# Alternating VectorE's steps over two batches in a four-stream decoder kernel, with gates spread straight from their column

## The reference

```python
def _layernorm(x, eps=1e-5):
    m, v = mean(x), var(x)
    return (x - m) / sqrt(v + eps)

# part "pick" (layer 0, ffn): half of the tokens are picked by their gates
gate = sigmoid((x @ Wg)[..., 0])
_, idx = top_k(gate, C)                       # C = 50 of 100
attn_in = take_along_axis(x, idx[..., None], axis=1)
...                                           # 16 heads over the 50 tokens
out = zeros_like(x).at[:, idx].set(o * gate_sel[..., None])

# part "quant" (layer 1, ffn)
x_norm = x * rsqrt(mean(square(x)) + 1e-6)
absmax = max(abs(x_norm), axis=-1)
scale = 127.0 / clip(absmax, 1e-5)
x_q = clip(round(x_norm * scale), -128, 127) / scale
y = einsum('bsd,od->bso', x_q, w_int8 * weight_scale) + bias

x = _layernorm(x + agent part(x))             # "mix"
x = _layernorm(x + cross attention(x, ctx))   # "first"
x = _layernorm(x + pick(x))                   # "pick"
x = _layernorm(x + banded attention(x))       # "local", 16 heads, band of 64
x = _layernorm(x + cross attention(x, ctx))   # "second"
x = _layernorm(x + quant(x))                  # "quant"
```

## Time and profile before

| | |
|---|---|
| Time, median of 3 runs (lowest to highest) | 1081.24 us (1078.39 to 1082.4) |
| Time of the profiled execution | 1081.67 us |
| Its span, first to last instruction | 1079.9 us |
| Mean granted TensorE clock over the span | 0.876 of 2.4 GHz |
| PE busy | 900.4 us (83%) |
| DVE busy | 704.7 us (65%) |
| ACT busy | 514.2 us (48%) |
| POOL busy | 371.4 us (34%) |

### The profile page before, as it was taken

How to read it: one execution, slowest core, us unless ns; L and a number is a source line. 1 busy time by engine, 2 the same in 40 slices (tenths; PEclk the granted TensorE clock), 3 DMA queues, 4 the chain that set the end, 5 groups by cost and what they waited for, 6 DMA issues and landing times.

```text
span 1079.9 us, 19738 instructions
## 1 busy us (share of the span) xinstructions
PE 900.4 (83%) x7022; PEld 671.0 (62%) x7022; DVE 704.7 (65%) x2081; ACT 514.2 (48%) x2392; POOL 371.4 (34%) x528
## 2 busy tenths in 40 slices
PE   7957798898798699998889788897979688997983
PEld 5735677565577587665567566574647466765662
DVE  4235666565777857567697876558487686766576
ACT  3102244766542345865433355664535144556641
POOL 0045401344463322254443422236144232223243
PEclk9766898999888799997889699898869898998896
DMA  7801400002214000002032200011030400000000
GB/s 227 285 32 44 157 1 2 2 8 85 92 55 144 24 1 2 2 23 73 30 123 75 78 9 2 12 69 34 11 102 1 144 17 1 1 2 1 1 1 31
DMA packets 23382, 54.10 MB, mean 50 GB/s; under 512 B 3696, under 2 KB 9588, under 8 KB 23284
## 3 DMA queue, kind: packets, MB, share of 16 engines
q1 hardware_dynamic: 23284, 52.84, 14.7%
HBM read 49.53 MB, written 3.31 MB: 49 GB/s over the span
## 4 chain that ended last, share of the span: by engine, by line
PE 50%; DVE 26%; ACT 10%; POOL 5%; issue 4%; DMA 4%; SPq 1%; DVEq 0%; POOLq 0%; ACTq 0%
PE psum L419 8%; PE psum L424 8%; PE psum L458 7%; ACT work L763 4%; PE psum L444 4%; DVE bn L878 4%; PE psum L578 4%; PE psum L589 3%; ACT work L728 3%; DVE x L885 3%; PE psum L599 2%; DVE mx L1040 2%; PE psum L581 2%; DVE res L945 1%; DVE mv L880 1%
## 5 line engine op out<-in xcount | busy, mean ns | idle before, releaser
L763 ACT ACTIVATE work<-psum,mx 100x100 f32<-100x100 f32 x512 | 169.8, 369 | 53.1 <-DVE mx L1040 52.8
L1124 POOL TENSOR_SCALAR ve<-mv 100x2 f32<-100x2 f32 x96 | 21.7, 226 | 289.7 <-DVE mv L880 289.4
L763 ACT ACTIVATION_READ_ACCUMULATOR work<-psum,mx 100x1 f32 x512 | 118.5, 232 | 0.0
L657 ACT ACTIVATE xT<-psum 128x100 f32<-128x100 f32 (+3 forms) x144 | 53.0, 374 | 124.5 <-PE psum L594 55.9
L458 PE MATMUL psum<-eT,ctx 128*128 128x100 f32 x768 | 103.6, 292 | 7.0 <-DVE eT L914 6.7
L458 PEld LDWEIGHTS psum<-eT,ctx 128*128 128x128 f32 x768 | 99.6, 207 | 10.5 <-DVE eT L914 8.9
L1153 POOL COPY work<-rden 100x128 f32<-100x128 f32 (+1 forms) x80 | 25.1, 314 | 201.4 <-DVE rden L1044 172.6
L444 PE MATMUL psum<-ctxT,qT 128*100 128x361 f32 x256 | 92.6, 508 | 2.1 <-ACT qT L657 1.2
L657 ACT ACTIVATE eT<-psum 100x400 f32<-100x400 f32 (+3 forms) x128 | 64.1, 513 | 49.1 <-PE psum L617 21.2
L878 DVE BATCH_NORM_STATS2 bn<-res 100x6 f32<-100x256 f32 x192 | 82.1, 427 | 6.6
L1040 DVE TENSOR_REDUCE mx<-psum 100x4 f32<-100x400 f32 x128 | 66.9, 565 | 26.4 <-PE psum L581 26.2
(11 more groups left out here) (231 smaller groups left out, 2066.3 us busy)
## 6 DMA issues: line engine op xcount, KB each, us to landing
ctx<-in_ctx SPq DMA_DIRECT2D x16, 768.0 KB, 7.0
ctxT<-in_ctxT SPq DMA_DIRECT2D x16, 722.0 KB, 4.3
cell<-in_cell SPq DMA_DIRECT2D x16, 282.0 KB
seq<-in_seq SPq DMA_DIRECT2D x16, 282.0 KB
x<-in_x SPq DMA_DIRECT2D x16, 200.0 KB
eT<-agent_rows SPq DMA_DIRECT2D x16, 200.0 KB
out<-xplus SPq DMA_DIRECT2D x16, 200.0 KB
work<-in_x SPq DMA_DIRECT2D x4, 400.0 KB
```

Of the source, the lines that this page charges most:

```text
L657: return e.activation(dst, src, ACT.Copy, **kw)
L763: last = e.activation(s.e[:, h, :], bk[g][0:S, q * S:(q + 1) * S], ACT.Exp, bias=s.mx[0:S, h:h + 1], accum_out=s.den[0:S, h:h + 1])
```

## The change

- `NORM` becomes r0 r1 bn0 bn1 ag0 ag1 x0 x1: `stats` is called once for both batches. In first and second, the yield stands behind r0, and the second step holds r1 and both batches' statistics.
- The diagonals dg0 and dg1 go. PE makes the row of gates as a product of the gate column, repeated over 100 columns as the stationary operand, with the identity: two matmuls of 100 columns in the place of one of 200. They wait for gt.
- Each batch has its own half of the tile `tie`; the order is tie0 tie1 rk0 rk1, and the rank's sum overwrites its tie.
- In pick, PE gathers ahead of transposing the selection, and ACT copies xT out ahead of the selection. The product k, which writes the bank where the transposed selection lies, waits for that copy.
- In quant, 1/127 moves into the clip, so that the reciprocal gives sc directly and ra goes; up and yq are made for each batch (four steps on 100x256 in the place of two on 100x512), and PE transposes batch 0 as soon as yq0 is there. The tile qscale and its one product go.
- All five order strings are new. The number of letters is the same on each engine. Of PE's 816 letters 72 stand for the same step of the same stream and turn as before; the mean move is 5.6 places, the largest 22. On DVE 63 of 752 are the same, with a mean move of 5.1 places. Stream A's last step on DVE moves from place 708 to 694 and B's from 750 to 734; C's and D's stay 751 and 752.

The diff, cut to its core (the strings are left out):

```diff
-NORM = "r0 bn0 ag0 r1 bn1 ag1 x0 x1"
+NORM = "r0 r1 bn0 bn1 ag0 ag1 x0 x1"
...
-                s.diag = s.eT[0:S, 0:T].rearrange("p (b t) -> p b t", b=NB)
-                s.tie, s.above = s.eT[0:S, T:T + S], s.eT[0:S, T + S:T + 2 * S]
+                s.tie = s.eT[0:S, 0:T].rearrange("p (b t) -> p b t", b=NB)
...
-                e.wait_ge(*dve("dg1", t))
-                e.matmul(bk[0][0:S, 0:T], ones[0:S, :], s.diag[:, :, :].rearrange("p b t -> p (b t)"),
-                         start=True, stop=True).then_inc(*pe.up("gates"))
+                e.wait_ge(*dve("gt", t))
+                for b in range(NB):
+                    last = e.matmul(bk[0][0:S, b * S:(b + 1) * S], s.gate[:, b:b + 1].to_broadcast([S, S]), ident[0:S, 0:S],
+                                    start=True, stop=True)
+                last.then_inc(*pe.up("gates"))
...
                     last.then_inc(*pe.up(name))
+                    if name == "q":
+                        e.wait_ge(*act("selT", t))
...
-            def stats(dve, t, b):
-                e.wait_ge(*dve(f"r{b}", t))
-                e.bn_stats(s.bn[:, b, :], s.res[0:S, b, :]).then_inc(*dve.up(f"bn{b}"))
-                e.wait_ge(*dve(f"bn{b}", t))
-                e.bn_aggr(s.mv[:, b, :], s.bn[:, b, :]).then_inc(*dve.up(f"ag{b}"))
+            def stats(dve, t):
+                for b in range(NB):
+                    e.wait_ge(*dve(f"r{b}", t))
+                    e.bn_stats(s.bn[:, b, :], s.res[0:S, b, :]).then_inc(*dve.up(f"bn{b}"))
+                for b in range(NB):
+                    e.wait_ge(*dve(f"bn{b}", t))
+                    e.bn_aggr(s.mv[:, b, :], s.bn[:, b, :]).then_inc(*dve.up(f"ag{b}"))
...
-                    stats(dve, t, b)
-                    yield
+                    if b == 0:
+                        yield
+                stats(dve, t)
+                yield
...
                 for b in range(NB):
-                    e.tensor_scalar(s.diag[:, b, :], ident[0:S, 0:S], s.gate[:, b:b + 1], None, ALU.mult).then_inc(
-                        *dve.up(f"dg{b}"))
...
+                    e.scalar_tensor_tensor(s.tie[:, b, :], bk[0][0:S, b * S:(b + 1) * S], s.gate[:, b:b + 1], before[:, :],
+                                           ALU.is_equal, ALU.mult).then_inc(*dve.up(f"tie{b}"))
+                for b in range(NB):
                     e.wait_ge(*dve(f"tie{b}", t))
+                    e.scalar_tensor_tensor(s.tie[:, b, :], bk[0][0:S, b * S:(b + 1) * S], s.gate[:, b:b + 1], s.tie[:, b, :],
+                                           ALU.is_gt, ALU.add, accum_out=s.rank[:, b:b + 1]).then_inc(*dve.up(f"rk{b}"))
...
-                e.reciprocal(s.ra[:, :], s.am2[:, :]).then_inc(*dve.up("ra"))
-                e.wait_ge(*dve("ra", t))
-                e.tensor_scalar(s.sc[:, :], s.ra[:, :], 127.0, None, ALU.mult).then_inc(*dve.up("sc"))
+                e.reciprocal(s.sc[:, :], s.am2[:, :]).then_inc(*dve.up("sc"))
...
-                e.tensor_scalar(s.prod[:, :, :], s.prod[:, :, :], ROUND, ROUND + 127.0, ALU.add, ALU.min).then_inc(*dve.up("up"))
+                for b in range(NB):
+                    e.wait_ge(*dve(f"y{b}", t))
+                    e.tensor_scalar(s.prod[:, b, :], s.prod[:, b, :], ROUND, ROUND + 127.0, ALU.add, ALU.min).then_inc(
+                        *dve.up(f"up{b}"))
+                for b in range(NB):
+                    e.wait_ge(*dve(f"up{b}", t))
+                    e.tensor_scalar(s.yq[:, b, :], s.prod[:, b, :], ROUND - 128.0, ROUND, ALU.max,
+                                    ALU.subtract).then_inc(*dve.up(f"yq{b}"))
```

More of the change, by code:

```diff
@@ L63, in up @@
         return self.sem, 1
-NORM = "r0 bn0 ag0 r1 bn1 ag1 x0 x1"
+NORM = "r0 r1 bn0 bn1 ag0 ag1 x0 x1"
 TENSOR = {
     "first": "xT q s0 s1 pT0 pT1 av0 av1 out0 out1",
-    "pick": "gates selT gath q k v hs0 hs tr0 tr1 av fo sc0 sc1",
+    "pick": "gates gath selT q k v hs0 hs tr0 tr1 av fo sc0 sc1",
     "local": "xT q k v0 v1 " + " ".join(f"s{i} tra{i} trb{i} R{i} av{i}" for i in range(NB * NC)) + " out0 out1",
@@ L77 @@
     "first": "xT q cb0 cb1 ex0 ex1 pT1 aT0",
-    "pick": "ez selT xT q vs0 ex0 ex1 eT0 rT fo",
+    "pick": "ez xT selT q vs0 ex0 ex1 eT0 rT fo",
     "local": "xT q v0 " + " ".join(f"exa{i} exb{i} eT{i} R{i}" for i in range(NB * NC)),
@@ L86 @@
     "first": "mx0 nb0 mx1 nb1 pT0 rs aT1 " + NORM,
-    "pick": "z0 z1 gp gt dg0 dg1 tie0 rk0 tie1 rk1 pk0 pk1 kT vs1 mx0 mx1 rd eT1 aT " + NORM,
+    "pick": "z0 z1 gp gt tie0 tie1 rk0 rk1 pk0 pk1 kT vs1 mx0 mx1 rd eT1 aT " + NORM,
     "local": "k0 k1 v1 " + " ".join(f"ma{i} mb{i} rd{i} eT{i} aT{i}" for i in range(NB * NC)) + " " + NORM,
     "second": "mx0 nb0 mx1 nb1 pT0 rs aT1 " + NORM,
-    "quant": "am am2 am3 ra sc y0 y1 up yq os " + NORM,
+    "quant": "am am2 am3 sc y0 y1 up0 up1 yq0 yq1 os " + NORM,
 }
@@ L484, in tensor_turns @@
                 last.then_inc(*pe.up("gath"))
+                for b in range(NB):
+                    last = e.transpose(bk[1][:, b * S:(b + 1) * S], s.pick[:, b, :], ident[0:S, 0:S])
+                last.then_inc(*pe.up("selT"))
                 yield
@@ L611, in tensor_turns @@
                 pe, act, dve, pool = s.at("quant")
-                e.wait_ge(*dve("yq", t))
                 half = bk[0].bitcast(BF16)
-                for c in range(NC):
-                    for b in range(NB):
+                for b in range(NB):
+                    e.wait_ge(*dve(f"yq{b}", t))
+                    for c in range(NC):
                         at_ = (c * NB + b) * S
@@ L706, in scalar_turns @@
                 yield
+                e.wait_ge(*pe("gath", t))
+                copy(s.xT[:, :, 0:P], bk[0][:, 0:NC * P].rearrange("p (c m) -> p c m", c=NC)).then_inc(*act.up("xT"))
                 e.wait_ge(*pe("selT", t))
                 copy(s.pickT[:, :, :].rearrange("p b t -> p (b t)"), bk[1][:, 0:T]).then_inc(*act.up("selT"))
-                e.wait_ge(*pe("gath", t))
-                copy(s.xT[:, :, 0:P], bk[0][:, 0:NC * P].rearrange("p (c m) -> p c m", c=NC)).then_inc(*act.up("xT"))
                 yield
@@ new lines @@
+        "AADCDBACBDCAABCABDCDBBBCDBCCADDADBDDDBABABCAABACBABDDABCACACDABACBADCCADACBCDCDABADDBDDABBAACABCABDC"
+        "CBDBACDABBCBDCABCADACBAABCABADDDBCCBBCBDDACBDCDBCACDBDCBCDBBCBCDBBBDCDCDCDCDBDBCDCDDCDCCDCDDDCDCCDCD"
+        "CCCDCDCDDDDDCCDD"),
+    "DVE": (
+        "AAABBAABAACCBBCAABAABDACDCACDBBCABABCBCADCBCDACDDCADBBDBDDCABACDCDABACCDBDABDACACADBCBADABACBCADBCAB"
+        "DCABACBDAABDCADCBACBDBADACBCDBACBDACDBACADBCADACACBDBABDAACCADBCDDBBCDBAABDABACCACADCBDCADACBBADCCBD"
+        "CADDDBBDBCACACBBACBDCABBCBADCCDBDAACBBCABADBDCADDBCDDCDABABDCDAADABCABDABADADBCABCBAABCDADBCABCBABAC"
+        "ABDCDABCAABBDCBADADACBDCACADACDABBCBDBCDBBCCBADABCABDACAADAADCACBDCABBDDCBDCCDAACACCBBDBDADCABCCBBDC"
+        "ADBBABDCDCDABCDBABBCACCDCCDDBACDABCAACBDADBCADDCBADDBADDBDCDACBABAABCDADBCDBACBDDCABACBADBADCABACBBA"
+        "DBACDABCDADCABABCADBDBCBBDCABACDABBACDAACCBADABABDABCDCAADACDDBCBDACBDBDCADBCBDCBBABCBDDACDCBABDADBA"
+        "CDCCBDACDDADACBACCBABADDCCADCABDCDCDABCDABCDDABADBCCABCBDBCDAABACDBACABDCABAABDCABDCDBCBDCACDABBCBDB"
+        "CDBCBDCBDBBDCDCDCBDCDCDCDCDDDCCCCBDDCDCCDCDDDCDDCDCD"),
```

83 lines of the change are left out of this document (28 added, 55 removed).

## The result

The changed kernel takes 1002.8 us (median of four runs, 997.1 to 1013.5) against 1081.1 us for the kernel before on the same chip: the ratio is 0.9265, with a 95% interval of 0.9226 to 0.9304. That is 78 us faster; 1060 was forecast, with 1040 as the low end. The profiled execution took 997.1 us with a span of 995.3 us, 84.6 less than the span before.

What follows compares the result with a forecast made beforehand. TensorE was taken as the fullest engine (86%), with VectorE the bound in bursts. The terms summed to 33.7 us, the other bound gave 14.8; 22 was taken off 1081.7, giving 1060 us, range 1040 to 1081.

Steps and rivals of the forecast that it cites:

- low end: Fastest time of the forecast's range, 1040 us: 1081 less 33.7 and 7 or 8 of the clock's 9.
- The statistics: VectorE's normalisation statistics, 96 times: alternating the batches saves 0.5 us each, 21.5 us on the chain after a discount.
- no overlap: Rival, chance 0.05: independent VectorE instructions wait for each other, so statistics and ranks gain nothing; 1076 us.
- Ranks and gather: Two terms, 16 times each: VectorE's ties together, 3.0 us; TensorE's gather ahead of the selection's transposes, 1.6 us.
- The gates: Gates, 16 times: VectorE loses two 0.27 us instructions and TensorE waits for gt instead of dg1; 3.8 us.
- The quantisation: Quantised layer, 16 times: sc's separate step goes, rounding and clamping are split by batch; 3.8 us.
- The sum: All terms together: 33.7 us if this chain stayed the longest, 14.8 by the other bound, 22 taken.
- up to 9 us more on the good side: TensorE's clock: fewer waits push it up, a hundredth of the mean clock being 2% of the 905 us.
- The order strings: New step order on all engines: taken as 0, with 10 us to either side.
- TensorE and ScalarE take it all: Rival, chance 0.15: VectorE gets idle but the waits move on, leaving 5 us; 1077 us.
- The end with two streams: Rival, chance 0.12: strings drain A and B early, and the end and the middle lose more than is gained; 1086 us.
- What would show it: Signs: DVE busy some 640 us, smaller `bn_stats` share, shorter waits at line 414 and the gates, clock at or above 0.876.

Runs made afterwards that it cites:

- e5: Kernel before, own order strings, with only the alternated statistics r0 r1 bn0 bn1 ag0 ag1: 23 us faster, 15 to 31 by the ratio's interval.
- e7: Changed kernel with the old order of ties and ranks, and the selection transposed and copied ahead of the gather again: 5 us slower, intervals overlapping.
- e4: Changed kernel with the old gates, diagonals on VectorE and one product of 200 columns: 16.5 us slower.
- e9: Kernel before, its own strings, with only the new gates and no diagonals: 7 us faster, 3.5 to 11 by the interval.
- e10: Changed kernel in which VectorE makes the two diagonals again and nothing waits for or reads them: 11.5 us slower.
- e6: Changed kernel with the quantised layer's steps of before: 1002.4 us against 1002.8.
- e2: Changed kernel's step edits with the five order strings of before: 38 us faster than the kernel before.
- e8: Kernel before with 16 unread bf16 matmuls at each of 80 places where TensorE waits for VectorE: 8 us slower.
- e1: Kernel before with the five new order strings and no instruction changed: 1049.6 us, 31 us faster.
- e13: Kernel before with only some loads for the last turn issued sooner in SP's string: ratio 0.993, 8 us faster.
- e11: Kernel before with the new strings on the four computing engines and SP's old string: 8 us faster.

## Why the prediction was wrong

**The statistics** were rightly sized: 0.45 us saved for 0.5, and 23 us alone (e5, 15 to 31) for the term's 21.5. What the trace said of independent instructions holds for `bn_stats` too: the pair at 309.86 lasts 0.74 us, so the second starts 0.33 after the first. The Trainium skill, "VectorE: DVE Perf Modes", section "The DRAIN you can't avoid", says that the next operation waits for the pipeline to empty, and adds that one which isn't held starts earlier; these runs show the second. The rival *no overlap* (1076) fell with it.

**Ranks and gather** agree with their 4.6: 5 us (e7), but the noise is as large.

**The gates** were undersized in the new order: 16.5 us (e4) for 3.8; alone they are 7 (e9), whose interval reaches down to the term. The weak step is "VectorE loses two instructions of 0.27 us", of which only what TensorE waits for was counted, with half of that on the path. The two instructions stand in VectorE's queue ahead of all three other streams' steps, and e10 shows that this alone, 9.1 us of them, costs 11.5.

**The quantisation** was taken at 3.8; no difference was measured (e6), though the instructions take what was forecast. The term's half on the path was an assumption, and the noise of e6 can't refute it.

**The sum** is the step that failed. "33.7 us if this chain stayed the longest to the end" was taken for a ceiling, and 22 for the value, for "TensorE's work is the same" and "TensorE being at 86% already". The work is the same, but not its length: TensorE's busy time falls by 24.5 us in e2 and by 43.9 in the changed kernel. At the low clock it is busy for 210.8 us before, 173.6 in e2 and 124.0 after; halved, the differences are 18.6 us and 43.4. The prediction had this term, at about the right price, and took it as "up to 9 us more on the good side", that is, for a clock that rises by a hundredth. It rose by 0.043, which at the prediction's own 9 us for each hundredth is 39. Hence the low end at 1040, too. As an estimate, if all of it lies on the path, the 18.6 us leave 19 of e2's 38, and 19 is near the 22 that was forecast: without strings and clock the sum was about right.

**Which waits lower the clock** stays open. That the fillers raise it (e8) shows that it follows what TensorE does in its waits. Counted from the records of TensorE between the first turn's first step and 20 us before the end, waits of 2 us and more go from 18 before (58 us) to 14 in e2 (39 us), 9 in e1 (31 us) and 3 after (11 us). But the clock falls 27 times in this stretch before and still 15 times after, and of these 15 at least 12 have no such wait since the fall before them. In e5 the long waits get fewer as well, 12 with 39 us, and the clock stays. Long waits alone don't explain it.

**The order strings** were taken as "0, with 10 us to either side"; they give 31 (e1). This is the second part of what failed. "They have no row" was wrong in one respect: the loads at 798 and 850 us have rows, and with 7.2 and 10.8 us they are 18 of the 43 us that the chain's DMA share of 4% stands for. Loads in time are worth 8 us in the old order (e13), the placing of the computing steps 8 with the old loads (e11), and the other 16 need both. What shows in e1 is that VectorE is busy for 690.0 us with the instructions that took 704.7, that the long waits are halved, and that the clock is 0.901. Which moves do it stays open: no run sets one of the four computing engines' strings among the old ones of the others.

**Together.** 31 + 38 = 69, and 78 were measured. Undoing the parts one by one in the new order sums to 37 + 16.5 + 5 + 0 = 59, more than the 47 that the steps are worth there. That would fit strings laid for the new lengths, of which each undoing spoils the fit; but the noise of such a sum is larger than the 12 us between them, and no run separates this.

**The rivals.** *TensorE and ScalarE take it all* (1077): ScalarE's share of the chain did grow, 10% to 13%, and line 590 waits 16.7 us for exponentials where line 589 waited 13.8, but the head's waits (line 522, now 523) fell by more, 15.5 to 10.7. *The end with two streams* (1086): the last 20 us have TensorE at 4.4 us of busy time and a clock of 0.63, where it was 3.2 and 0.54. It cost nothing. The earlier trace rows were read a little too strongly: VectorE's lines there add up to 79% of the ten microseconds, not to "nearly the whole chain".

**What would show it.** DVE at 640.5 for 640, `bn_stats` under 4%, line 414's wait (411 now) down by 36%, the gates' at 4.1 us, the clock above 0.876: all came true. They test the mechanism and not its worth; none would have told 1060 from 1003. The one that would, TensorE's busy time, wasn't on the list.

## What to carry to other kernels

A chain's share is no ceiling for a gain where the busiest engine's speed depends on being kept busy: estimate the matmuls' time at the low clock as well (here TensorE is busy for 211 of 900 us at it) and what half of it would give back. An instruction on a queue shared by several streams has a price there whoever reads its output: the unread diagonals cost about their own length, 11.5 us for 9.1, with some 7 us of noise. An order of steps is to be judged with the lengths for which it was laid and with its loads: the same strings gave 31 us, or 8 with late loads.

## What the runs showed of the hardware

- 80 us of additional matmuls in TensorE's waits (e8) lengthen the kernel by 8 us. The score matmul of 361 columns goes from 508 to 483 ns, as the clock goes from 0.876 to 0.911. The low level isn't a matter of a kernel's beginning: it is a quarter of the time before (268 of 1080 us) and a sixth after (161 of 995). The Trainium skill, "TensorE: Matmul & The Clock Gate", section "HAM oscillation — how this bites in real kernels", tells of a kernel whose clock falls again and again, each time that TensorE waits for a load; the trace agrees that it falls again and again, 27 times over the turns before, though TensorE itself waits for no load in them.
- A score matmul of 361 columns takes 811 ns on average at the low level and 467 at the high one (line 444 before).
- 9.1 us of VectorE work that nobody reads cost 11.5 us (e10), with some 7 us of noise.
- VectorE's instructions took 704.7 us in one order and 690.0 in another (e1). The pair on 100x128 at line 980 took 2.09 us at 317.73 and 0.48 at 115.37 in the same run. Beside the slow pair GpSimd ran two instructions on 100x512 (1.27 us each, from 317.25 and 318.47); no run singled out whether they slowed it.
